# Layer 1's gathered rows in fp32 instead of three bf16 parts, in a two-layer graph network

## The chip, the cores and the metric

The kernel runs on one core of one Trainium2 chip. The metric is the device time of one execution, in microseconds (us), lower is better. Before the change it is 3567.8 us, the median of three runs (3565.1 to 3599.5). The core has a matrix engine (TensorE, PE in the profile, with its weight loads as PEld), a vector engine (VectorE, DVE), a scalar engine (ScalarE, ACT), GpSimd (POOL) and SyncE (SP), which issues transfers. Each works through its own list of instructions in order and waits for the others on semaphores.

## The reference, cut to what matters

There are 6250 nodes with 128 features each and 200,000 edges, sorted by their target node `dst`. The targets are drawn so that low node numbers have many edges.

```
h = relu(layernorm(x))
x = x + layer0(h, edges, edge_attr, edge_weight)     # a small network on each edge, summed by dst, + h
h = relu(layernorm(x))
agg = segment_sum(h[src], dst)                        # layer 1: the sum of the source rows of each node
x = x + relu(relu((h + agg) @ W1 + b1) @ W2 + b2)
```

The change lies in `agg` of layer 1 alone: a row of `h` is fetched for each edge and the rows of the edges that end at one node are added up.

## The kernel before

**Layout.** Edges go in blocks of 512 (4 tiles of 128), two blocks make a pair, four pairs a body (`RING = 4`). Node features lie as `nodes` and `xs`, 128 partitions by 49 tiles by 128 features (fp32); seven groups of seven tiles (`NG`, `GT`) are worked one after the other where whole arrays are passed over. `acc` holds the sums by node.

**Layer 0** takes the first 2575 us. In each pair GpSimd gathers 8 tiles of 128 rows from `table0` (fp32, 512 bytes a row) into the ring `big`; TensorE multiplies, VectorE adds, and the pair's messages are summed with a one-hot matrix `hot` in a product of fp32 operands (line 771: stationary 128x128 messages, 64 moving columns, the one-hot tile read as F32). Beside it counts of edges are made for dense windows (line 792).

**Between the layers** (lines 1239 to 1280 of VectorE, 655 to 675 of ScalarE, 836 to 855 of TensorE) the new `x` is formed, its layer norm made, and then, group by group:

- ScalarE writes the seven tiles of `nodes` (line 668, semaphore `normed1`), then copies the group to bf16 as the first part (line 675, `parts_first`); for the third group and later it waits until an earlier group's store has landed, as `parts` has two slots.
- VectorE subtracts that part (line 1268, `left_made`), GpSimd casts the remainder to bf16 as the second part (line 558), VectorE subtracts again and writes the third part in bf16 (line 1273, `parts_made`). The three parts add up to the fp32 value.
- TensorE transposes the group (line 850) and VectorE copies it to `acc` (line 1271, `acc1_made`).
- SyncE stores the parts as the group's rows of `table1`, 768 bytes a row (line 463).

GpSimd's gathers of layer 1 begin once all stores have landed (line 560) and `slot1_free` has its first four counts, which TensorE gives at line 855, after the last copy to `acc`.

**Layer 1's loop.** Nodes below 2880, with many edges each, are summed from the counts: `row_sums` (line 875) multiplies 49 tiles of `nodes` with counts, fp32, 49 products each time. The other edges, 16 bodies or 64 pairs, go by gathers. GpSimd gathers a pair (line 525, eight indirect transfers) when `slot1_free` says that TensorE is done with the pair four before (line 563). VectorE makes the pair's one-hot tiles (line 1061). TensorE's `sum_rows` (line 865) then multiplies each of the 8 gathered tiles with its one-hot tile: three bf16 products a tile, 24 a pair, each a weight load of 128x128 and 64 moving columns. VectorE adds the two sums to `acc` (line 1288), and makes the next pair's one-hot tiles only after that, as there is one set of them.

The order is written out by hand. A step of the loop over `k` (lines 897 to 907 and 1332 to 1342) has two bodies, so eight pairs, called slots t = 0 to 7. After its `sum_rows`, TensorE does in slots 0, 1 and 5 one `row_sums`; in slots 2 and 3 three windows of counts each, in slots 4, 6 and 7 two each (line 792, four bf16 products of 500 columns a window or more). Each window waits for one-hot tiles that VectorE makes in the same slot (lines 1133 and 1136), with room for half a window ahead of TensorE's. There are seven such steps, ahead of them one body with its own order (lines 890 to 896) and behind them one body of four pairs with nothing between the sums (lines 909 to 911). SyncE loads the indices of a later pair once a gather has landed (lines 466 to 472).

The last part multiplies with W1 and W2 and stores `out`.

Of the kernel before, what the change touches and what calls it, by code (L numbers as in the profile page):

```python
# [5 lines left out]
F32 = mybir.dt.float32  # L6
F32R = mybir.dt.float32r
BF16 = mybir.dt.bfloat16
F16 = mybir.dt.float16
I32 = mybir.dt.int32  # L10
ALU = mybir.AluOpType
ACT = mybir.ActivationFunctionType
AX = mybir.AxisListType

P = 128
D = 128
# [7 lines left out]
GT = 7  # L24
NG = NT // GT
N_PAD = NT * P
# [3 lines left out]
TB = 4  # L30
BLK = TB * P
RING = 4
NPAIR = -(-N_EDGES // (2 * BLK * RING)) * RING
NBODY = NPAIR // RING
NB = 2 * NPAIR
# [9 lines left out]
NBJ = NB // NBP  # L45
# [37 lines left out]

NP3 = 3


def gnn_program(nc, x, ea, ew, src, src_tiles, dst_tiles, dst_blocks, We1, be1, We2, be2, Wt, bt, Wn1, bn1, Wn2, bn2,
                W1, b1, W2, b2, out):
    ctx = ExitStack()
    with ctx:  # L90
        def sb(name, shape, dt=F32):
            return ctx.enter_context(nc.sbuf_tensor(name, shape, dt))

        def sem(name):
            return ctx.enter_context(nc.semaphore(name))

        def dram(name, shape, dt=F32):
            return nc.dram_tensor(name, shape, dt, kind="Internal").ap()


        table0 = dram("table0", (N_PAD, D))
        table1 = dram("table1", (N_PAD, NP3 * D), BF16)
        base_d = dram("base_d", (NB,), I32)
# [8 lines left out]
        nodes = sb("nodes", [P, NT, D])  # L112
# [49 lines left out]
        def one_hot_tiles(words, n):  # L162
# [34 lines left out]
        RROW = RING * 2 * TB * D  # L197
        big = sb("big", [P, RROW * NP3 // 2])
        assert RROW * NP3 // 2 == RROW + 2 * 2 * TB * D
        rows = big[:, 0:RROW].rearrange("p (u q t d) -> p u q t d", u=RING, q=2, t=TB)  # L200
        msg = big[:, RROW:RROW + 2 * 2 * TB * D].rearrange("p (m q t d) -> p m q t d", m=2, q=2, t=TB)
        rows1 = big[:, :].bitcast(BF16).rearrange("p (u q t i d) -> p u q t i d", u=RING, q=2, t=TB, i=NP3)

        parts = big[:, 0:2 * GT * D * NP3 // 2].bitcast(BF16).rearrange("p (s t i d) -> p s t i d", s=2, t=GT, i=NP3)
        left = big[:, GT * D * NP3:GT * D * NP3 + GT * D].rearrange("p (t d) -> p t d", t=GT)
        ef = sb("ef", [P, 2, BLK])
# [4 lines left out]
        half_at = RROW + 2 * TB * D - GT * D  # L211
        stages, stages2 = ([a[:, 0:GT * D].rearrange("p (t d) -> p t d", t=GT) for a in pair] for pair in (
            (big[:, RROW + 2 * TB * D:], big[:, half_at:]),
            (ef[:, :, :].rearrange("p q c -> p (q c)"), big[:, half_at - GT * D:])))
        assert NBJ * BLK + 2 * NB <= half_at - GT * D and GT * D * (NP3 + 1) <= RROW + 2 * TB * D

# [6 lines left out]
        hot = sb("hot", [P, 2, 2, TB, W], F32R)  # L223
        hot_sum = sb("hot_sum", [P, 2, 2, W], F32R)
        hot1 = hot[:, 0, 0, :, :].rearrange("p t w -> p (t w)").bitcast(BF16).rearrange("p (q t w) -> p q t w", q=2, t=TB)

# [7 lines left out]
        p_agg = ps[:, 7 * BANK:7 * BANK + 4 * W].rearrange("p (q s w) -> p q s w", q=2, s=2)  # L234
# [31 lines left out]
        table0_stored = sem("table0_stored")  # L266
        table1_stored = [sem(f"table1_stored{s}") for s in (0, 1)]

# [29 lines left out]
        normed1 = sem("normed1")  # L298
# [23 lines left out]
        rows_added = sem("rows_added")  # L322
        parts_first = sem("parts_first")
        left_made = sem("left_made")
        parts_second = sem("parts_second")
        parts_made = sem("parts_made")

# [39 lines left out]
        def _(sp):  # L367
# [35 lines left out]
            sweeps, start, total, bodies = load_params(sp)  # L403
# [57 lines left out]
            for g in range(NG):  # L461
                sp.wait_ge(parts_made, g + 1)
                sp.dma_start(t1[:, g * GT:(g + 1) * GT, :], parts[:, g % 2].rearrange("p t i d -> p t (i d)"))\
                  .then_inc(table1_stored[g % 2], 16)

# [33 lines left out]
        def _(pool):  # L499
# [30 lines left out]
            def gather_pair(table, to, u, landed):  # L530
                for q in (0, 1):
                    gather_block(table, to, u, q, landed)
# [3 lines left out]

            def to_rows1(u, q, t):
                return rows1[:, u, q, t].rearrange("p i d -> p (i d)")

            pool.wait_ge(table0_stored, 16 * NG)  # L540
# [14 lines left out]
            pool.tensor_copy(keys1, keys0).then_inc(keys_moved, 1)  # L555
            for g in range(NG):
                pool.wait_ge(left_made, g + 1)
                pool.tensor_copy(parts[:, g % 2, :, 1, :], left).then_inc(parts_second, 1)
            for s in (0, 1):
                pool.wait_ge(table1_stored[s], 16 * ((NG + 1 - s) // 2))  # L560
            with pool.Fori(0, total) as b:
                for u in range(RING):
                    pool.wait_ge(slot1_free, b * RING + u + 1)
                    pool.wait_ge(idx1_loaded[u], b * 16 + 16)
                    pool.sem_inc(pairs_begun, 1)
                    gather_pair(table1, to_rows1, u, gathered1)


        @block.scalar
        def _(act):  # L570
# [94 lines left out]
            for g in range(NG):  # L665
                for u in range(GT):
                    t = g * GT + u
                    i = act.activation(nodes[:, t, :],
                                       xs[:, t, :], ACT.Relu,
                                       bias=shift[:, t:t + 1], scale=rstd[:, t:t + 1])  # L670
                i.then_inc(normed1, 1)
                act.wait_ge(normed1, g + 1)
                if g >= 2:
                    act.wait_ge(table1_stored[g % 2], 16 * (g // 2))
                act.activation(parts[:, g % 2, :, 0, :], nodes[:, g * GT:(g + 1) * GT, :], ACT.Copy).then_inc(parts_first, 1)

# [35 lines left out]
        def _(pe):  # L712
# [144 lines left out]
            def sum_rows(b, u):  # L857

                n = b * (2 * RING) + 2 * u
                pe.wait_ge(hot1_made, n + 2)  # L860
                for q in (0, 1):
                    pe.wait_ge(gathered1[u][q], b * (16 * TB) + 16 * TB)
                    for t in range(TB):
                        for p in range(NP3):
                            i = pe.matmul(p_agg[:, q, 0, :], rows1[:, u, q, t, p, :], hot1[:, q, t, :],  # L865
                                          start=(t == 0 and p == 0), stop=(t == TB - 1 and p == NP3 - 1))
                i.then_inc(slot1_free, 1)
# [67 lines left out]
        def _(dve):  # L935
# [328 lines left out]
            for g in range(NG):  # L1264
                dve.wait_ge(parts_first, g + 1)
                if g:
                    dve.wait_ge(parts_made, g)
                dve.tensor_tensor(left, nodes[:, g * GT:(g + 1) * GT, :], parts[:, g % 2, :, 0, :], ALU.subtract)\
                   .then_inc(left_made, 1)
                dve.wait_ge(turned1, g + 1)  # L1270
                dve.tensor_copy(acc_group(g), p_turn[g % 2]).then_inc(acc1_made, 1)
                dve.wait_ge(parts_second, g + 1)
                dve.tensor_tensor(parts[:, g % 2, :, 2, :], left, parts[:, g % 2, :, 1, :], ALU.subtract)\
                   .then_inc(parts_made, 1)
            chain(dve.tensor_scalar(dense_edges, dst_t[:, :], float(C_NODES), -float(2 * N_PAD), ALU.is_lt, ALU.mult))
# [133 lines left out]
```

## Time and profile before

| | |
|---|---|
| median of three runs | 3567.8 us (3565.1 to 3599.5) |
| span of the profiled execution, first to last instruction | 3560.6 us |
| layer 0, to the last addition to `acc` | about 2575 us |
| layer 1's gathers, first to last | 2649.2 to 3501.8 us |
| TensorE busy | 2710.7 us, 76% |
| GpSimd busy | 2066.6 us, 58% |
| VectorE busy | 1969.1 us, 55% |
| mean granted TensorE clock | 0.80 of full speed |

The profile gives no whole time for the profiled execution beside its span; the median of the runs is 7.2 us above the span, and the fastest run 4.5 us. Busy shares are means over stages with different limits, so each stage is read by itself. One fp32 product of the program is two MATMUL and two LDWEIGHTS records in the trace (49 products of line 875 are 98 records), a bf16 product is one of each. A few records are missing. "Issue" in a wait means that the engine waited for nothing the profile shows.

### The profile page before, as it was taken

The numbers are of one execution on the slowest core, as the hardware profiler recorded it, in microseconds if no ns is written. First come the engines' busy times: TensorE is split into PE (matmuls) and PEld (weight loads), VectorE is DVE, ScalarE is ACT, GpSimd is POOL, SyncE is SP. The second block draws the span as 40 slices with busy tenths as digits, with TensorE's granted clock in tenths as the row PEclk, the third lists the DMA queues.
The fourth block names the chain that finished last, engine by engine and source line by source line (L and its number), as shares of the span: only waits on it lengthen the run. The fifth ranks groups of instructions, "written<-read, shape, count | busy, mean of one in ns | idle before, by whom it ended". The sixth has DMA issues, their size and how long they took to land. (4 is left out here: it accounts for less than half of the span.)

```text
span 3560.6 us, 56685 instructions
## 1 busy us (share of the span) xinstructions
PE 2710.7 (76%) x14584; PEld 1629.8 (46%) x14585; DVE 1969.1 (55%) x4112; ACT 1005.8 (28%) x1000; POOL 2066.6 (58%) x2104
## 2 busy tenths in 40 slices
PE   4677888788688888887888788887845767766777
PEld 2444444444344444444444444444432545544554
DVE  7655566565556666666666666676673333233333
ACT  3233333333333333333333333332241111111111
POOL 4666666656566666666666666655325556555552
PEclk8788888888888877888888888988765777777777
DMA  5444444444444444444444444434222434334332
GB/s 189 110 124 129 130 127 126 133 114 133 114 128 120 130 126 123 127 123 124 126 131 124 121 126 124 124 109 119 34 105 88 134 118 130 120 98 128 119 104 60
DMA packets 229238, 424.69 MB, mean 119 GB/s; under 512 B 82704, under 2 KB 141585, under 8 KB 229073
## 3 DMA queue, kind: packets, MB, share of 16 engines
q0 software_dynamic: 74752, 153.23, 18.4%
q1 hardware_dynamic: 103152, 177.42, 15.1%
q10 hardware_dynamic: 51266, 93.34, 7.5%
q8 instruction: 18, 0.29, 0.0%
q14 instruction: 50, 0.40, 0.0%
HBM read 364.35 MB, written 59.43 MB: 119 GB/s over the span
## 5 line engine op out<-in xcount | busy, mean ns | idle before, releaser
L525 POOL DMA_INDIRECT big<-table,idx x2080 | 2042.4, 982 | 1360.7 <-issue 670.2
L792 PE MATMUL ps<-nodes 128*128 128x500 bf16 x1280 | 467.5, 489 | 266.3 <-issue 170.5
L771 PE MATMUL ps<-hot,big 128*128 128x64 f32 x3136 | 419.0, 284 | 134.8 <-issue 111.1
L751 PE MATMUL ps<-arena,we 128*128 128x512 f32 x784 | 507.0, 778 | 14.2 <-issue 5.1
L604 ACT ACTIVATE big<-big 128x1024 f32<-128x1024 f32 x196 | 207.1, 1057 | 946.3 <-DVE big L1085 723.3
L771 PEld LDWEIGHTS ps<-hot,big 128*128 128x128 f32 x3136 | 402.4, 203 | 145.4 <-issue 143.0
L1136 DVE TENSOR_SCALAR nodes<-iota_k,win_off,nodes 128x500 bf16<-128x500 f16 x1280 | 454.7, 406 | 10.2 <-issue 10.1
L792 PEld LDWEIGHTS ps<-nodes 128*128 128x128 bf16 x1280 | 106.0, 109 | 520.1 <-issue 289.9
L1085 DVE TENSOR_TENSOR big<-ps,big 128x1024 f32<-128x1024 f32 x196 | 239.1, 1220 | 179.6 <-remote 121.3
L594 ACT ACTIVATE arena<-ps,cols 128x1024 f32<-128x1024 f32 x196 | 218.3, 1114 | 375.6 <-PE ps L743 160.4
L681 ACT ACTIVATE arena<-ps 128x490 f32<-128x490 f32 x96 | 100.0, 1041 | 754.6 <-PE ps L795 593.8
L1133 DVE TENSOR_TENSOR nodes<-iota_b,nodes 128x384 bf16<-128x384 f16 (+1 forms) x492 | 245.2, 498 | 112.6 <-remote 65.9
L627 ACT ACTIVATE arena<-ps 128x490 f32<-128x490 f32 x192 | 199.2, 1037 | 363.4 <-remote 345.4
L1105 DVE SCALAR_TENSOR_TENSOR arena<-ps,cols,arena 128x1024 f32<-128x1024 f32 x98 | 125.3, 1279 | 278.8 <-remote 262.8
L1078 DVE TENSOR_TENSOR acc<-ps,acc 128x128 f32 x392 | 113.7, 290 | 298.2 <-remote 237.9
L875 PE MATMUL ps<-acc,nodes 128*128 128x120 f32 x1568 | 221.5, 296 | 72.4 <-issue 65.2
L792 PE MATMUL ps<-arena 128*128 128x500 bf16 x384 | 171.9, 558 | 132.3 <-DVE arena L1136 92.7
L1133 DVE TENSOR_TENSOR arena<-iota_b,arena 128x256 bf16<-128x256 f16 x192 | 80.7, 421 | 317.1 <-PE ps L792 173.1
L743 PE MATMUL ps<-arena,we 64*128 64x512 f32 x784 | 233.5, 666 | 23.1 <-DMA win_row<-win_d 20.2
L875 PEld LDWEIGHTS ps<-acc,nodes 128*128 128x128 f32 x1568 | 207.4, 212 | 82.9 <-issue 82.6
L751 PEld LDWEIGHTS ps<-arena,we 128*128 128x128 f32 x784 | 171.3, 243 | 158.5 <-issue 153.7
L599 ACT ACTIVATE arena<-arena,cols 128x1024 f32<-128x1024 f32 x196 | 241.0, 1229 | 0.0
(139 smaller groups left out, 2577.0 us busy)
## 6 DMA issues: line engine op xcount, KB each, us to landing
arena<-in_ew SPq DMA_DIRECT2D x196, 512.0 KB
arena<-in_ea SPq DMA_DIRECT2D x196, 256.0 KB
counts_d<-arena ACTq DMA_DIRECT2D x192, 245.0 KB
acc<-counts_d ACTq DMA_DIRECT2D x15, 2940.0 KB
big<-table,idx POOLq DMA_INDIRECT x2080
table<-big SPq DMA_DIRECT2D x7, 672.0 KB, 3.0
idx<-in_src SPq DMA_DIRECT2D x260, 4.0 KB
xs<-in_x SPq DMA_DIRECT2D x7, 448.0 KB, 8.3
```

The source lines that it names most:

```text
L525: pool.indirect_dma_start(to(u, q, t), None, table, bass.IndirectOffsetOnAxis(ap=idx[:, u, at:at + 1], axis=0))\
L594: act.activation(hid[:, :, :].rearrange("p q c -> p (q c)"), p_hid2, ACT.Relu, bias=be1_c).then_inc(hid_made, 2)
L599: act.activation(v, v, ACT.Sigmoid, bias=bt_c, scale=wt_c).then_inc(tw_made, 2)
L604: act.activation(v, v, ACT.Relu).then_inc(msg_made, 2)
L743: pe.matmul(p_hid[q], we1[k, :], ea_s[k, u, :], start=True, stop=True).then_inc(hid_mm, 1)
L751: pe.matmul(p_ef[q], we2[:, :], hid[:, q, :], start=True, stop=True).then_inc(ef_mm, 1)
L771: pe.matmul(p_agg[:, q, 0, :], msg[:, m, q, t, :], hot_f[:, m, q, t, :], start=(t == 0), stop=(t == TB - 1))
L792: m = pe.matmul(to, hots[:, t, :], keys[:, t, :], start=False, stop=True, skip_group_check=True)
L875: m = pe.matmul(to, nodes[:, a, :], sums[:, :, a, :], start=(a == 0), stop=(a == NT - 1))
L1085: dve.tensor_tensor(msg[:, u % 2, :, :, :].rearrange("p q t d -> p (q t d)"), p_pre2, rows[:, u, :, :, :].rearrange("p q t d -> p (q t d)" ...
L1133: dve.tensor_tensor(hots[:, h * half:h * half + n, :], iota_v.to_broadcast([P, n, P]), half_src.to_broadcast([P, n, P]), ALU.is_equal)
L1136: m = dve.tensor_scalar(keys[:, h * half + t, :], iota_k[:, :], win_off[:, bass.ds(win, 1)], key[:, h * n + t:NTILE + VP][:, bass.ds(at, 1 ...
```

## The change

`table1` becomes fp32 with 512 bytes a row, and SyncE stores each group of `nodes` to it as soon as `normed1` says that it is written. ScalarE's copy to bf16, VectorE's two subtractions and GpSimd's cast are gone, with four semaphores, and the two store semaphores are one. GpSimd gathers fp32 rows into the same ring as layer 0. The one-hot tiles of layer 1 are fp32-sized (the tile `hot`, half of it), and `sum_rows` makes one fp32 product a tile, 8 a pair, with the same operands in form as line 771.

```diff
-        table1 = dram("table1", (N_PAD, NP3 * D), BF16)
+        table1 = dram("table1", (N_PAD, D))
...
-        hot1 = hot[:, 0, 0, :, :].rearrange("p t w -> p (t w)").bitcast(BF16).rearrange("p (q t w) -> p q t w", q=2, t=TB)
+        hot1 = hot[:, 0, :, :, :]
...
             for g in range(NG):
-                sp.wait_ge(parts_made, g + 1)
-                sp.dma_start(t1[:, g * GT:(g + 1) * GT, :], parts[:, g % 2].rearrange("p t i d -> p t (i d)"))\
-                  .then_inc(table1_stored[g % 2], 16)
+                sp.wait_ge(normed1, g + 1)
+                sp.dma_start(t1[:, g * GT:(g + 1) * GT, :], nodes[:, g * GT:(g + 1) * GT, :]).then_inc(table1_stored, 16)
...
-            for g in range(NG):
-                pool.wait_ge(left_made, g + 1)
-                pool.tensor_copy(parts[:, g % 2, :, 1, :], left).then_inc(parts_second, 1)
-            for s in (0, 1):
-                pool.wait_ge(table1_stored[s], 16 * ((NG + 1 - s) // 2))
+            pool.wait_ge(table1_stored, 16 * NG)
...
-                    gather_pair(table1, to_rows1, u, gathered1)
+                    gather_pair(table1, to_rows, u, gathered1)
...
-                act.wait_ge(normed1, g + 1)
-                if g >= 2:
-                    act.wait_ge(table1_stored[g % 2], 16 * (g // 2))
-                act.activation(parts[:, g % 2, :, 0, :], nodes[:, g * GT:(g + 1) * GT, :], ACT.Copy).then_inc(parts_first, 1)
...
-                        for p in range(NP3):
-                            i = pe.matmul(p_agg[:, q, 0, :], rows1[:, u, q, t, p, :], hot1[:, q, t, :],
-                                          start=(t == 0 and p == 0), stop=(t == TB - 1 and p == NP3 - 1))
+                        i = pe.matmul(p_agg[:, q, 0, :], rows[:, u, q, t, :], hot1[:, q, t, :].bitcast(F32),
+                                      start=(t == 0), stop=(t == TB - 1))
...
             for g in range(NG):
-                dve.wait_ge(parts_first, g + 1)
-                if g:
-                    dve.wait_ge(parts_made, g)
-                dve.tensor_tensor(left, nodes[:, g * GT:(g + 1) * GT, :], parts[:, g % 2, :, 0, :], ALU.subtract)\
-                   .then_inc(left_made, 1)
                 dve.wait_ge(turned1, g + 1)
                 dve.tensor_copy(acc_group(g), p_turn[g % 2]).then_inc(acc1_made, 1)
-                dve.wait_ge(parts_second, g + 1)
-                dve.tensor_tensor(parts[:, g % 2, :, 2, :], left, parts[:, g % 2, :, 1, :], ALU.subtract)\
-                   .then_inc(parts_made, 1)
```

## Rows read from the trace of the kernel before

**Rows 1.** Windows, three steps of layer 1's loop: us, PE, PEld, DVE, ACT, POOL, clock, DMA, GB/s.

```profile
2852.00:2955.00 103.00, 73.76 (x545) 51.06 (x546) 34.23 (x106) 12.04 (x12) 60.78 (x64) 0.73 0.38 114
2955.00:3060.00 105.00, 73.95 (x576) 52.51 (x573) 35.19 (x110) 12.95 (x13) 63.10 (x67) 0.73 0.41 126
```

**Rows 2.** Groups by line, layer 1's seven steps (2740 to 3496 us): busy, mean | idle before.

```profile
L525 POOL DMA_INDIRECT big<-table,idx x449 | 429.7, 957 | 327.3 <-issue 126.8 <-PE ps L865 119.8 <-remote 80.7
L865 PE MATMUL ps<-hot,big 128*128 128x64 bf16 x1344 | 75.0, 225 | 46.5 <-issue 26.2 <-DVE hot L1061 19.5
```

**Rows 3.** The chain of waits, 2968 to 3076 us, shares by line.

```profile
by line: PE ps L875 37.0%; issue 27.6%; PE ps L865 7.1%; PE ps L792 7.1%; DVE arena L1136 6.6%; DVEq L1116 4.2%; DVEq L1070 2.9%; DVEq L1133 2.5%; DVE arena L1133 1.5%; DVE hot L1061 1.3%; DVEq L1136 1.2%; DVE acc L1288 0.9%; DVEq L1140 0.6
```

**Rows 4.** Timeline of PE, one step: start, length, line, operands, count [idle before, releaser].

```profile
2969.19 1.46 PE L865 MATMUL ps<-hot,big 128*128 128x64 bf16 x24 [3.56 <-DVE hot L1061]
2970.46 12.56 PE L875 MATMUL ps<-arena,nodes 128*128 128x120 f32 x90
...
2986.45 0.86 PE L865 MATMUL ps<-hot,big 128*128 128x64 bf16 x24 [0.46 <-issue]
2987.14 11.18 PE L875 MATMUL ps<-acc,nodes 128*128 128x120 f32 x98
...
3008.59 1.46 PE L865 MATMUL ps<-hot,big 128*128 128x64 bf16 x24
...
3013.24 1.01 PE L792 MATMUL ps<-arena 128*128 128x500 bf16 x2 [3.08 <-issue]
...
3027.23 2.02 PE L792 MATMUL ps<-arena 128*128 128x500 bf16 x4 [4.20 <-DVE arena L1136]
...
3060.34 1.99 PE L792 MATMUL ps<-arena 128*128 128x500 bf16 x4 [1.53 <-issue]
```

**Rows 5.** Timeline of POOL in layer 1: gathers that follow a pair's last.

```profile
2988.12 0.94 POOL L525 DMA_INDIRECT big<-table,idx  x1 [3.40 <-PE ps L865]
...
2993.66 0.95 POOL L525 DMA_INDIRECT big<-table,idx  x1 [0.30 <-issue]
...
3014.31 1.05 POOL L525 DMA_INDIRECT big<-table,idx  x1 [2.38 <-remote]
```

**Rows 6.** Timeline of PE in layer 0, the fp32 product of line 771 and what follows it.

```profile
92.68 2.72 PE L771 MATMUL ps<-hot,big 128*128 128x64 f32 x16
95.20 0.25 PE L774 MATMUL ps<-hot_sum,ones 128*1 128x128 f32 x1
...
1501.00 1.90 PE L771 MATMUL ps<-hot,big 128*128 128x64 f32 x16
1502.71 0.25 PE L774 MATMUL ps<-hot_sum,ones 128*1 128x128 f32 x1
...
2571.77 3.02 PE L771 MATMUL ps<-hot,big 128*128 128x64 f32 x16 [1.56 <-DVE hot L1091]
2574.55 0.35 PE L774 MATMUL ps<-hot_sum,ones 128*1 128x128 f32 x1
```

**Rows 7.** Windows: granted clock (third from the end) around slots 0 and 1.

```profile
2963.00:2975.00 12.00, 7.92 (x50) 6.18 (x51) 3.01 (x11) 1.25 (x2) 7.40 (x8) 0.50 0.26 67
2975.00:2985.00 10.00, 8.63 (x76) 8.62 (x75) 0.94 (x3) 0.00 (x0) 7.56 (x8) 0.99 0.27 69
```

**Rows 8.** Timeline of all engines, from the first normalised group to the first gather.

```profile
2614.29 2.80 ACT L668 ACTIVATE nodes<-xs,shift,rstd 128x128 f32<-128x128 f32 x7 [0.78 <-DVE shift L976]
...
2640.18 1.76 PE L850 MATMUL ps<-ident,nodes 128*128 128x128 f32 x7 [2.02 <-ACT nodes L668]
...
2642.45 1.73 DVE L1271 COPY acc<-ps 128x896 f32<-128x896 f32 x1
2642.60 0.93 POOL L558 CAST big<-big 128x896 bf16<-128x896 f32 x1 [3.05 <-DVE big L1268]
2644.03 1.08 DVE L1273 TENSOR_TENSOR big<-big 128x896 bf16<-128x896 f32 x1
...
2649.18 0.97 POOL L525 DMA_INDIRECT big<-table,idx  x1 [5.65 <-issue]
```

**Rows 9.** Timeline of layer 1's last body: the first and the last pair's sums.

```profile
3510.76 0.87 PE L865 MATMUL ps<-hot,big 128*128 128x64 bf16 x24 [1.22 <-DVE hot L1061]
...
3518.81 1.46 PE L865 MATMUL ps<-hot,big 128*128 128x64 bf16 x24 [1.76 <-DVE hot L1061]
```

**Rows 10.** Groups by line: VectorE's one-hot tiles, layer 1's (256) and layer 0's (512).

```profile
L1061 DVE TENSOR_TENSOR hot<-ps,rel 128x256 bf16<-128x256 f32 x128 | 48.0, 416 | 22.4 <-issue 21.9 <-DVE ps L1278 0.3
L1091 DVE TENSOR_TENSOR hot<-ps,rel 128x512 fp32r<-128x512 f32 x6 | 4.1, 680 | 0.0
```

**Rows 11.** Timeline of POOL and PE in layer 0: a pair's first gather, and a slow stretch of TensorE.

```profile
1506.70 0.94 POOL L525 DMA_INDIRECT big<-table,idx  x1 [2.71 <-remote]
...
1562.59 1.34 PE L771 MATMUL ps<-hot,big 128*128 128x64 f32 x6 [0.50 <-issue]
```

More of the change, by code:

```diff
@@ L82 @@
 assert sum(SLOTS, ()) == tuple(range(CB))
-NP3 = 3
 def gnn_program(nc, x, ea, ew, src, src_tiles, dst_tiles, dst_blocks, We1, be1, We2, be2, Wt, bt, Wn1, bn1, Wn2, bn2,
@@ L197, in gnn_program @@
         RROW = RING * 2 * TB * D
-        big = sb("big", [P, RROW * NP3 // 2])
-        assert RROW * NP3 // 2 == RROW + 2 * 2 * TB * D
+        big = sb("big", [P, RROW + 2 * 2 * TB * D])
         rows = big[:, 0:RROW].rearrange("p (u q t d) -> p u q t d", u=RING, q=2, t=TB)
         msg = big[:, RROW:RROW + 2 * 2 * TB * D].rearrange("p (m q t d) -> p m q t d", m=2, q=2, t=TB)
-        rows1 = big[:, :].bitcast(BF16).rearrange("p (u q t i d) -> p u q t i d", u=RING, q=2, t=TB, i=NP3)
-        parts = big[:, 0:2 * GT * D * NP3 // 2].bitcast(BF16).rearrange("p (s t i d) -> p s t i d", s=2, t=GT, i=NP3)
-        left = big[:, GT * D * NP3:GT * D * NP3 + GT * D].rearrange("p (t d) -> p t d", t=GT)
         ef = sb("ef", [P, 2, BLK])
@@ L214, in gnn_program @@
             (ef[:, :, :].rearrange("p q c -> p (q c)"), big[:, half_at - GT * D:])))
-        assert NBJ * BLK + 2 * NB <= half_at - GT * D and GT * D * (NP3 + 1) <= RROW + 2 * TB * D
+        assert NBJ * BLK + 2 * NB <= half_at - GT * D
         dst_b = big[0:NBP, 0:NBJ * BLK].bitcast(I32).rearrange("p (j c) -> p j c", j=NBJ)
@@ L266, in gnn_program @@
         table0_stored = sem("table0_stored")
-        table1_stored = [sem(f"table1_stored{s}") for s in (0, 1)]
+        table1_stored = sem("table1_stored")
         ea_loaded = [sem(f"ea_loaded{u}") for u in range(RING)]
@@ L322, in gnn_program @@
         rows_added = sem("rows_added")
[L323 to L326, printed above, removed]
         hid2_mm = sem("hid2_mm")
@@ L535, in to_rows @@
                 return rows[:, u, q, t, :]
-            def to_rows1(u, q, t):
-                return rows1[:, u, q, t].rearrange("p i d -> p (i d)")
             pool.wait_ge(table0_stored, 16 * NG)
```

## The prediction, made before the result was known

> **What bounds the kernel now.** I read the share of busy time first and found no engine full, so the stage of the change has to be read by itself. The windows cut at layer 1's steps show about 105 us a step, with TensorE at 74, GpSimd at 61 to 63 and VectorE at 35 [rows 1]: again nobody is full, so the chain of waits and the timeline decide. GpSimd first, because the change touches its gathers. The grouped rows say that it waits 119.8 us for line 865, TensorE's sums of gathered rows [rows 2]; in the timeline it starts a pair's gathers 0.8 us after the sums that free the slot (sums from 2986.45 for 0.86 us, gather at 2988.12), and in the other pairs it is held back only by a gap of 2.4 us behind its own last gather [rows 4, 5]. It thus runs nearly a whole ring of four pairs ahead. Its floor is 8 gathers at 1.25 us (0.95 and a gap of 0.30) and 2.5 us between pairs, 12.5 us a pair or 100 us a step, 5 us under the present step. TensorE with VectorE sets the pace: on the chain of one step line 875 has 37.0%, "issue" 27.6%, line 865 and line 792 7.1% each [rows 3]. 7.1% of that window of 108 us is 7.7 us, and the sums are busy 75.0/7 = 10.7 us a step [rows 2], so about 70% of the sums' time is on the chain. That is the first sign of how much of a dearer sum will be felt.
>
> **Price of the fp32 sums.** Layer 0 has the very form that the change puts in: 128x128 fp32 stationary, 64 fp32 columns, the one-hot tile read as F32, 8 products or 16 records. I measure from its start to the start of what follows. At full clock (2.4 GHz) that is 1502.71 - 1501.00 = 1.71 us; at half (1.2 GHz) 2.52 (from 92.68) and 2.78 (from 2571.77), of which I take 2.6 [rows 6]. Three bf16 products a tile, 24 records, take 2987.14 - 2986.45 = 0.69 at full and 2970.46 - 2969.19 = 1.27 at half [rows 4]. So a pair gets dearer by **1.0 us at full and 1.3 at half clock** (ends: 1.0 and 1.5). Slot 0 lies in a stretch granted 0.50, and slot 1's follows one at 0.99 [rows 7].
> A rule of the Trainium skill speaks for a smaller price. The page "FP8 and Floating Point Precision", section "TensorE Precision Notes", says that a true fp32 product takes four passes through the array; against three bf16 products that would be 4/3 of the time. The row disagrees (1.71 against 0.69 is 2.5 times), so I hold to the row.
>
> **Where it is felt.** The order written out by hand decides it, slot by slot.
> - Slots 0, 1 and 5 have a row sum right behind, which waits for nothing (2970.46 and 2987.14 follow without a gap) [rows 4]: felt in full, 1.3, 1.0, 1.3.
> - Slots 2 and 6 have windows whose one-hot tiles VectorE has made during the row sum before: felt, 1.0 and 1.3. (That they are ready I read from the order, lines 1324 to 1326 against 898 to 907.)
> - In slots 3, 4 and 7 TensorE waits for VectorE behind the sums: 3.08, 4.20 and 1.53 us in this step [rows 4]. The smallest is over 1.3: felt at nothing. Without this cover it would cost 3 x 1.3 = 3.9 us a step.
> - In slot 0 the clock rises while TensorE works, and slot 1's row sum takes 11.18/98 = 114 ns a record, slot 0's, which begins at half clock, 12.56/90 = 140 [rows 4, 7]; a longer sum moves the row sum later, into the faster clock. I take 0.4 us off, ends 0 and 1.3.
> Sum: 1.3 + 1.0 + 1.0 + 1.3 + 1.3 - 0.4 = 5.5 us a step, **38.5 us** over seven. The last body has no cover: the first pair and the last run at 0.87 and 1.46 [rows 9], two pairs at each clock, 2 x 1.0 + 2 x 1.3 = 4.6. The first body I put at 1, between 0 (three of its sums are followed by waits for VectorE) and 5. Together **+44 us**.
>
> **The stage of the parts.** Now ScalarE's seven groups begin at 2614.29, the last third part is ready at 2644.03 + 1.08 = 2645.1 and the first gather starts at 2649.18, so a store takes 4.1 us to be seen [rows 8]. Afterwards ScalarE writes seven groups of 2.8 us without a stop and ends at 2633.9; plus 4.1 is 2638.0. The other condition of the gathers, TensorE's count of free slots, needs the last copy to `acc`: 2633.9, a transposition of 1.75 and the copy of 1.73, is 2637.4. What is late next is thus this copy, 0.6 us behind in line. Gain **11 us** at GpSimd. VectorE saves two subtractions of 1.08 a group and is 7.6 us earlier (2645.1 against 2637.5). The stored row sum that TensorE does first is stretched by the gathers beside it, so I take the 11, with 7.6 as the other end. Removed with it and off the chain: GpSimd's seven casts of 0.93, SyncE's stores shrink from 672 to 448 KB. SyncE now waits for `normed1` in place of `parts_made`; behind it stand only the next stores and later index loads, which need gathers to have landed. One store semaphore instead of two adds nothing.
>
> **Gathers and one-hot tiles.** A gather row shrinks from 768 to 512 bytes. GpSimd's time does not follow: 957 ns is its mean in layer 1 [rows 2], and layer 0 with 512-byte rows has 0.94 us and a gap of 2.71 between pairs [rows 11]. Nothing, as GpSimd is not the bound; if it became so, the same 12.5 us a pair. The one-hot tiles double in bytes, but VectorE writes 512 fp32 elements in 680 ns against 256 bf16 in 416 [rows 10], so the element costs 1.03 ns either way: nothing; the other end is 0.1 us a tile on the chain, 13 us over 128.
>
> **Slow stretches.** Beside gathers TensorE at times starts records some 0.7 us apart with no releaser ("issue"): 26.2 us in front of the sums in the seven steps [rows 2]. The sums' records fall by a third, 24 to 16; if each record costs its share, 9 us go. The lower end is nothing, and more is a rival below. I take **-9**.
>
> **The sum** is 44 - 11 - 9 = +24 us against the profiled span of 3560.6. The profile gives only this span, which lies 7.2 us under the runs' median; what lies around it does not change, so I add to the median: **3592 us**, +0.7%.
>
> **Rivals.**
> 1. *Every sum is felt* (ends slower). Place: slots 3, 4 and 7. If VectorE's windows do not start at their own time but as late after the sums as now, for example because both queues are slow at the same moment, the cover is none: 61 felt pairs at 1.35 are 82, and with a slow stretch that does not shrink, 82 - 11 = +71, **3639**. For it: the releaser of two of the three waits reads "issue" [rows 4], so their cause is not shown. Against: VectorE's windows do not wait for the sums in the code, and the chain has only 70% of line 865. It decides once more than 56 us of sums are felt, 47 if nothing else is saved. Chance 0.20.
> 2. *Sums at little price*, the rule of four passes as a mechanism here. 32 passes at the bf16 spacing would take 1.27 x 4/3 = 1.69 at half and 0.92 at full, +0.42 and +0.23: 1.7 a step, 12 in all, 1 for the last body, 13 - 11 - 9 = -7, **3561**. Against it stand all pairs of [rows 6]. Chance 0.12. (The page is the one named above.)
> 3. *Slow stretches follow the gathered bytes.* "Issue" is 27.6% of the chain [rows 3], 30 us a step. A third fewer bytes, a third fewer stalls: 10 a step, -70; 44 - 11 - 70 = -37, **3531**. Against: layer 0 gathers 512-byte rows, and there too a sum is torn apart by 0.50 us of "issue" and POOL has its 2.71 [rows 11]. It decides once 69 us of stalls go. Chance 0.13.
> That the product would not be fp32 at all is out: the operands are read as line 771's are, and that line shows two records a product.
> The forecast's own case: 0.55, from 3570 to 3612 (the ends of its terms).
>
> **Numbers.** What a measurement of this kernel can tell from no change is about 1%, 36 us: faster is under 3532, slower over 3603.5. Slower: rival 1 nearly whole and a third of my own case, 0.38. Faster: half of rival 3 and a little more, 0.08. The rest, 0.54, is within. The range for 8 in 10 leaves out the far half of rivals 1 and 3: **3548 to 3640**.
>
> **What would show it.** The sums at 1.9 us at full and about 2.8 at half clock in place of 0.86 and 1.46; the first gather 24 us behind ScalarE's first normalised group instead of 35; steps of 109 to 111 us; waits of TensorE for VectorE behind slots 3, 4 and 7 shrunk to between 0 and 3 us; GpSimd waiting longer for line 865. Wrong it would be with steps at 105 or under (rivals 2 and 3), with sums at 1.2 and 1.7 us (rival 2), or with those waits at their old length behind a longer sum (rival 1).

## The result and the profile after

The changed kernel takes **3641.8 us**, the median of four runs (3627.9 to 3654.5), beside 3566.5 for the kernel before (four runs). The ratio is 1.016, with a 95% interval of 1.011 to 1.022: slower, by 1.1 to 2.2%. The profiled execution has a span of 3652.7 us and is the slowest of the four, so a sum made from this trace overstates the median by some 13 us. The line numbers are 22 or 23 lower now: line 865 became 842, 875 became 852, 792 became 770.

I cut both traces at the same events. To ScalarE's first copy of `acc`, layer 0 takes 2581.7 us instead of 2575.8, which the change does not touch: +5.9. From there to the first gather 61.9 instead of 73.4: -11.5. From the first gather to the row sum that closes the first body 103.8 instead of 99.3: +4.5. From there to the start of the last row sum, which is seven steps, 832.4 instead of 747.6: **+84.8**, or 106.8 to 118.9 a step. The rest 72.9 instead of 64.6: +8.3. Together +92, the difference of the spans.

The groups of TensorE by line in the seven steps come first of the kernel before, where [rows 2] has the sums, then of the changed one (busy, mean of one | idle time before).

```profile
L875 PE MATMUL ps<-acc,nodes 128*128 128x120 f32 x1470 | 203.4, 294 | 44.2 <-issue 43.4
L792 PE MATMUL ps<-arena 128*128 128x500 bf16 x348 | 153.9, 552 | 116.0 <-DVE arena L1136 78.4 <-issue 37.3
L875 PE MATMUL ps<-arena,nodes 128*128 128x120 f32 x686 | 90.9, 295 | 6.6 <-issue 6.5
```

```profile
L852 PE MATMUL ps<-acc,nodes 128*128 128x120 f32 x1470 | 222.2, 315 | 55.3 <-issue 55.0
L842 PE MATMUL ps<-hot,big 128*128 128x64 f32 x896 | 161.3, 356 | 35.6 <-DVE hot L1038 29.1 <-issue 6.1
L770 PE MATMUL ps<-arena 128*128 128x500 bf16 x348 | 145.4, 528 | 84.4 <-DVE arena L1113 74.8 <-issue 9.1
L852 PE MATMUL ps<-arena,nodes 128*128 128x120 f32 x687 | 105.6, 318 | 18.8 <-issue 18.5
```

The sums went from 75.0 to 161.3 us busy, +86.3. The waits ahead of the windows gave 31.6 back and those ahead of the sums 10.9, and the windows themselves took 8.5 less. But the row sums, whose instructions nobody changed, took 33.5 us more of busy time and 23.3 more of waiting. That is the part no term of mine held.

One line of GpSimd and the chain of one step show who bounds the loop now. GpSimd waited 245.0 us for the sums instead of 119.8 [rows 2]: it has more slack, not less. In the chain the sums have 12.9% of 109 us, 14.1 us, instead of 7.7 [rows 3].

```profile
L514 POOL DMA_INDIRECT big<-table,idx x451 | 430.7, 955 | 410.4 <-PE ps L842 245.0 <-issue 129.6 <-remote 35.8
```

```profile
by line: PE ps L852 35.7%; issue 19.1%; PE ps L842 12.9%; DVE arena L1113 5.8%; PE ps L770 5.6%; DVEq L1047 3.8%; DVEq L1093 3.6%; DVE arena L1110 2.1%; DVE hot L1038 1.9%; DVEq L1113 1.7%; DVEq L1110 1.6%; DVE acc L1257 1.1%; DVEq L1102 1.
```

VectorE's one-hot tiles are not dearer in fp32, 416 ns each as in bf16 [rows 10]:

```profile
L1038 DVE TENSOR_TENSOR hot<-ps,rel 128x256 fp32r<-128x256 f32 x112 | 42.0, 416 | 21.6 <-issue 21.6
```

Then the sums themselves, in the timeline of TensorE after the change (start, length, ...). At full clock 16 records take 1.90 us, as I had read in layer 0 [rows 6]. At half clock they take 3.67, and 3.47 from their start to the start of what follows (3050.42 to 3053.89), where I had put 2.6.

```profile
3003.40 1.90 PE L842 MATMUL ps<-hot,big 128*128 128x64 f32 x16
3005.13 11.15 PE L852 MATMUL ps<-acc,nodes 128*128 128x120 f32 x98
...
3039.22 3.67 PE L842 MATMUL ps<-hot,big 128*128 128x64 f32 x16 [0.54 <-DVE hot L1038]
...
3045.80 1.99 PE L770 MATMUL ps<-arena 128*128 128x500 bf16 x4 [2.79 <-DVE arena L1113]
...
3050.42 3.67 PE L842 MATMUL ps<-hot,big 128*128 128x64 f32 x16
3053.89 10.44 PE L852 MATMUL ps<-acc,nodes 128*128 128x120 f32 x70
```

The rows from 3039 to 3046 show the cover at work: where TensorE waited 4.20 us for VectorE behind slot 4's bf16 sums [rows 4] it now waits 2.79 behind longer ones.

Last the start of the stage. The first gather comes 23.5 us behind the first normalised group (2643.65 - 2620.12) instead of 34.9 [rows 8]:

```profile
2620.12 18.96 ACT L650 ACTIVATE nodes<-xs,shift,rstd 128x128 f32<-128x128 f32 x49 [0.78 <-DVE shift L953]
...
2640.93 1.74 DVE L1243 COPY acc<-ps 128x896 f32<-128x896 f32 x1 [0.95 <-PE ps L828]
...
2643.65 2.50 POOL L514 DMA_INDIRECT big<-table,idx  x1 [55.73 <-PEq L833]
```

It was released by TensorE's count of free slots (line 833), which follows the last copy to `acc`, and not by the stores: this copy is indeed what is late next.

### The profile page after: what moved, and what is told of

The parts are those of the page before. It is cut to its first block, busy times and chain, and to the rows that moved or that the text cites. A ratio compares the mean times of both kernels' runs of the same rounds, so it can differ in the third digit from the quotient of the medians.

```text
span 3652.7 us, 55621 instructions
## 1 busy us (share of the span) xinstructions
PE 2817.5 (77%) x14072; PEld 1767.6 (48%) x14073; DVE 1959.1 (54%) x4098; ACT 997.7 (27%) x993; POOL 2056.8 (56%) x2097
## 4 chain that ended last, share of the span: by engine, by line
PE 36%; issue 19%; DVE 16%; DVEq 14%; another core or an unknown queue 13%; DMA 1%; ACT 1%; SPq 0%; ACTq 0%
PE ps L852 10%; PE ps L770 7%; PE ps L729 6%; DVE nodes L1113 5%; DVEq L1047 4%; PE ps L842 3%; PE ps L738 3%; PE ps L749 3%; DVEq L1093 3%; DVE hot L1068 2%; PE ps L721 2%; DVEq L1110 2%; DVEq L1113 2%; DVE arena L1113 2%
## 5 line engine op out<-in xcount | busy, mean ns | idle before, releaser
L770 PE MATMUL ps<-nodes 128*128 128x500 bf16 x1280 | 458.0, 480 | 271.3 <-issue 156.3
L729 PE MATMUL ps<-arena,we 128*128 128x512 f32 x784 | 496.3, 764 | 15.1 <-DVE arena L1082 5.6
L852 PE MATMUL ps<-acc,nodes 128*128 128x120 f32 x1568 | 239.4, 315 | 79.1 <-issue 74.1
L852 PEld LDWEIGHTS ps<-acc,nodes 128*128 128x128 f32 x1568 | 228.2, 231 | 87.5 <-issue 87.2
L738 PEld LDWEIGHTS ps<-wn1b,arena 128*128 128x128 f32 x1568 | 191.0, 197 | 115.0 <-issue 112.7
## 6 DMA issues: line engine op xcount, KB each, us to landing
counts_d<-arena ACTq DMA_DIRECT2D x192, 245.0 KB
```

The costliest lines, as they stand in the source:

```text
L729: pe.matmul(p_ef[q], we2[:, :], hid[:, q, :], start=True, stop=True).then_inc(ef_mm, 1)
L738: i = pe.matmul(p_pre[q][:, t * D:(t + 1) * D], efs[m][:, q, t * P:(t + 1) * P], wn1b[:, :], start=True, stop=True)
L770: m = pe.matmul(to, hots[:, t, :], keys[:, t, :], start=False, stop=True, skip_group_check=True)
L852: m = pe.matmul(to, nodes[:, a, :], sums[:, :, a, :], start=(a == 0), stop=(a == NT - 1))
```

## The experiments

All twelve kernels ran on three other chips, four on each, beside the kernel before on the same chip. There the kernel before takes 2899 to 2909 us and not 3567. GpSimd's eight gathers of a pair follow each other at 1.25 us with no gap of 2.4 us between pairs, and TensorE has next to no "issue" in front of its row sums (see the groups below). What makes the first chip's executions have these stretches was not found, and none of the twelve runs below was made on it. The prices of the product and of the cover could be measured all the same, on a loop without stalls.

**1 to 4: which part costs, and in which slots.** The first kernel undoes the product alone in the changed kernel:

```diff
-                        i = pe.matmul(p_agg[:, q, 0, :], rows[:, u, q, t, :], hot1[:, q, t, :].bitcast(F32),
-                                      start=(t == 0), stop=(t == TB - 1))
+                        for p in range(3):
+                            i = pe.matmul(p_agg[:, q, 0, :], hot1b[:, q, 0:2, :].rearrange("p t w -> p (t w)"), hot1b[:, q, t, :],
+                                          start=(t == 0 and p == 0), stop=(t == TB - 1 and p == 2))
```

> The changed kernel with three bf16 products a gathered tile again (24 a pair, 128x128 stationary, 64 columns); the stage of the parts stays away and the gathers stay at 512 bytes. Left out: the products read a one-hot tile as stationary operand in place of the gathered rows, so the sums of layer 1 are not the reference's. Theory A (all of the loss is the fp32 product): 3555 us, the old kernel less the 11 us of the stage that is gone. Theory B (the loss lies in the gathers, the one-hot tiles or the new start of the stage): stays over 3600.

Measured: 2896.8 us beside 2908.7, ratio 0.996 (0.994 to 0.997), **12 us faster** than the kernel before. The stage's gain is what I predicted, 11, and the smaller gathers leave no room for another effect. Theory B falls for the gathers and the stage. The fp32 one-hot tiles go with the fp32 product in every kernel here, so these runs do not part the two; the 416 ns above do.

The second does the product alone in the kernel before:

```diff
-                        for p in range(NP3):
-                            i = pe.matmul(p_agg[:, q, 0, :], rows1[:, u, q, t, p, :], hot1[:, q, t, :],
-                                          start=(t == 0 and p == 0), stop=(t == TB - 1 and p == NP3 - 1))
+                        i = pe.matmul(p_agg[:, q, 0, :], rows_f[:, u, q, t, 0:D], hot1[:, q, t, :].bitcast(F32),
+                                      start=(t == 0), stop=(t == TB - 1))
```

> The old kernel with its stage of parts and 768-byte rows, and one fp32 product a tile (it reads the first 512 bytes of a row of parts as fp32, so the sums are not the reference's). Theory A: 3567 + 86 (the whole measured loss of 75 and the 11 that the missing stage gave) = 3653 us. Theory B: near 3567.

Measured: 2989.0 us, ratio 1.026 (1.023 to 1.029), **+80 us**. Theory A stands: 768-byte rows and the parts stage are there and the loss is too. With the 12 us of the stage off, the two kernels give +68.

The third and fourth choose the product by slot (`if fp32` around the two forms, and the one-hot tiles to match). The diff is the third's; the fourth has `(0, 1, 2, 5, 6), True`, where `True` puts the fp32 product in the first and last body too:

```diff
+FP32_SLOTS, OUTER = (3, 4, 7), False
...
-                    sum_rows(k * 2 + (t // RING - 1), t % RING)
+                    sum_rows(k * 2 + (t // RING - 1), t % RING, t in FP32_SLOTS)
```

> As the kernel with bf16 products again, but the fp32 product in slots 3, 4 and 7 of the step alone (seven steps), where TensorE waited for VectorE behind the sums. Cover theory: an fp32 sum at half clock is 2.2 us dearer than the bf16 one, the waits were 3.1, 4.2 and 1.5 us, so 0.7 us a step is felt: 5 us over the kernel with bf16 products. Rival, every sum is felt: 3 x 2.2 x 7 = 46 us over it.

> The other part: fp32 products in slots 0, 1, 2, 5, 6 and in the first and last body, bf16 in slots 3, 4 and 7. Cover theory: nearly the whole loss, 75 to 80 us over the kernel with bf16 products. Rival, every sum is felt alike: 7 x (2 x 2.2 + 3 x 1.0) + 11 = 63 or less, about 40 under the changed kernel.

Measured: 2901.5 us for slots 3, 4, 7, which is 4.7 over the kernel with bf16 products everywhere, where the cover theory said 5 and its rival 46. And 2957.6 us for the others, 60.8 over it (57 by the ratios), less than the 75 to 80 of the cover theory and near the 63 of its rival. The two add up to 65 us. The cover theory thus holds for the third kernel and misses the fourth; the table below shows what it lacked.

**5 to 8: the changed kernel on such a chip, and two ways on.**

> The changed kernel itself, on the chip of these runs. On a chip where GpSimd needs 10 us a pair and the old kernel 2909 us, the parts measured so far add up: 57 (slots 0, 1, 2, 5, 6 and the outer bodies) + 5 (slots 3, 4, 7) - 13 (no stage of parts) = +49 us or 1.7%. If the slots' parts do not add (a wait moved from one slot to the next), it is 20 us or more off that.

Measured: 2969.5 us beside 2899.3, ratio 1.025 (1.023 to 1.027): **+70 us** and not 49. The slots' parts do not add; over the kernel with bf16 products it is some 83, by the medians 82, and the two parts gave 65. The next table says where. It holds the mean time from one slot's sums to the next slot's, over the seven steps, worked out from the timelines of TensorE:

```
slot                          0      1      2      3      4      5      6      7    step
first chip, before        15.04  17.51   8.50  12.47  10.24  19.41   6.98  16.82  107.0
first chip, after         20.61  17.59   8.74  13.86  10.35  25.32   6.27  16.39  119.1
bf16 products             13.49  11.81   7.61  10.77   7.72  13.50   5.38  12.91   83.2
fp32 in slots 3, 4, 7     13.37  11.75   7.62  11.29   8.31  13.06   5.34  12.99   83.7
fp32 in the others        15.74  12.73   8.48  10.72   7.72  15.87   6.28  13.06   90.6
changed kernel            16.11  12.73   8.47  11.34   8.35  16.90   6.27  13.11   93.3
```

In the last four rows each slot can be read by itself. Slots 1, 2 and 6 grow by 0.9, the price at full clock. Slots 3 and 4 grow by 0.6 and slot 7 by 0.2 where their sums grow by 2.2, 2.2 and 1.0: the cover holds most of it in every kernel. The traces show it directly: TensorE's waits inside these three slots are 2.20, 1.77 and 2.67 us in the mean with bf16 products and 0.67, 0.49 and 1.70 in the changed kernel. Slots 0 and 5 grow by 2.6 and 3.4. Slot 5 is where the parts do not add: -0.4 with fp32 in slots 3, 4 and 7, +2.4 with fp32 in slot 5 itself, +3.4 with both.

So the price of slots 3, 4 and 7 depends on what the others run. With bf16 in the others, fp32 in these three makes a step 0.5 us longer (83.2 to 83.7). With fp32 in the others it makes it 2.7 us longer (90.6 to 93.3), 19 us over the seven steps, and 1.4 of the 2.7 appear in slots 5 and 0.

The timelines of slot 5 show where. First the kernel with bf16 products, then the one with fp32 products in the others, slot 5 among them, then the changed one. The row sum of 98 records behind the sums takes 12.40, 12.29 and 13.60.

```profile
2396.63 1.46 PE L844 MATMUL ps<-hot 128*128 128x64 bf16 x24
2397.91 12.40 PE L854 MATMUL ps<-acc,nodes 128*128 128x120 f32 x98
2410.14 0.86 PE L844 MATMUL ps<-hot 128*128 128x64 bf16 x24
```

```profile
2408.00 3.68 PE L845 MATMUL ps<-hot,big 128*128 128x64 f32 x16
2411.47 12.29 PE L859 MATMUL ps<-acc,nodes 128*128 128x120 f32 x98
2423.60 1.90 PE L845 MATMUL ps<-hot,big 128*128 128x64 f32 x16
```

```profile
2401.25 3.67 PE L842 MATMUL ps<-hot,big 128*128 128x64 f32 x16
2404.72 13.60 PE L852 MATMUL ps<-acc,nodes 128*128 128x120 f32 x98
2418.16 1.90 PE L842 MATMUL ps<-hot,big 128*128 128x64 f32 x16
```

And the windows over the same three stretches, from the sums to the end of the row sum (granted clock third from the end): 0.87, 0.81 and 0.74 on average.

```profile
2397.00:2410.00 13.00, 13.00 (x118) 13.00 (x116) 3.16 (x10) 0.68 (x1) 9.81 (x11) 0.87 0.21 51
```

```profile
2408.00:2423.00 15.00, 15.00 (x109) 15.00 (x110) 3.16 (x10) 1.04 (x1) 11.34 (x13) 0.81 0.19 48
```

```profile
2401.00:2418.00 17.00, 16.97 (x115) 16.85 (x115) 3.35 (x11) 1.04 (x1) 12.37 (x13) 0.74 0.18 53
```

The clock is at half first and at full after that, so these shares tell when it rises: 3.8, 5.8 and 8.6 us after the start of slot 5's sums. The second kernel does what I had assumed with my 0.4 us off: its sums are 2.2 us longer, the clock rises 2.0 later, and in five of its seven steps the row sum is a little shorter than with bf16 sums (12.3 against 12.4 to 12.6); in the other two it took 12.7 and 13.8, so this is no fixed amount. In the changed kernel the sums of slot 5 are no longer than that, and yet the rise comes 2.8 us later still. What differs is slots 3, 4 and 7 before it. That their longer sums and shorter waits move the rise is thus shown; which of them does it, and why, was not tried.

The filler kernels put products whose results nobody reads where TensorE waits:

```diff
+            def fill(n):
+                for i in range(n):
+                    pe.matmul(ps[:, 4 * BANK:4 * BANK + CK], iota_b[:, :], iota_k[:, :], start=True, stop=True)
...
+                    if t in (3, 4, 7):
+                        fill(3)
                     for i in SLOTS[t]:
                         count_late(k, i)
+                    if t == 7:
+                        fill(7)
```

> The changed kernel with filler products (128x128 by 500 columns, 16 bit, result never read) where TensorE waited for VectorE: 3 behind the sums of slots 3, 4 and 7, and 7 ahead of slot 0. Theory (the sums of slots 0, 3, 4, 5, 7 cost 3.7 us and not 1.9 because the granted clock is half there): the clock stays up, those sums take 1.9, and it is 30 to 60 us faster than the changed kernel. Rival (the clock does not follow, or the fillers themselves are in the way): the fillers add up to 7 x 16 x 0.42 = 47 us less what the waits hide, 0 to 30 us slower.

> The same fillers in the old kernel. Its step is near GpSimd's floor on a chip with 10 us a pair: nothing, within 10 us. On a chip with 12.5 us a pair TensorE sets the pace and the sums cost only 1.27 against 0.69: 10 to 25 us faster if the clock follows.

Measured: 2962.4 us, ratio 1.022 (1.019 to 1.024), 7 us under the changed kernel. The two intervals overlap, but on this chip each run of the one (2954.8 to 2966.0) lies under each of the other (2968.6 to 2971.9). Neither the 30 to 60 us of the theory nor the rival's range holds it. The fillers gave 2884.1 us in the kernel before, ratio 0.995 (0.993 to 0.997), **15 us faster**, where I had expected nothing on such a chip. The clock follows in some places only. The sums of slots 4 and 5 stay at 3.67 in the mean, slot 0's go from 3.42 to 2.86. In a step where the clock has risen by then, slot 0's sums take 1.99, as here, where seven fillers at line 852 run in the wait:

```profile
2523.74 2.95 PE L852 MATMUL ps<-iota_k,iota_b 128*128 128x500 f16 x7
2527.01 1.99 PE L842 MATMUL ps<-hot,big 128*128 128x64 f32 x16 [0.32 <-DVE hot L1046]
2528.84 1.33 PE L856 MATMUL ps<-arena,nodes 128*128 128x120 f32 x10
```

In the mean slots 0 and 5 gain 1.0 and 1.1 us and slots 3 and 4, where the fillers run longer than the wait, lose 0.8 and 1.3 in the changed kernel. That a sum costs 1.90 us where the granted clock is 1.00 and 3.67 where it is 0.50 is shown by every kernel; that the half clock can be bought off with fillers at this price is not.

The next kernel splits each row into two bf16 parts instead of three. It leaves out the third part (and with it GpSimd's cast) and holds about 16 of the value's bits:

```diff
-NP3 = 3
+NP3 = 2
...
-                dve.tensor_tensor(left, nodes[:, g * GT:(g + 1) * GT, :], parts[:, g % 2, :, 0, :], ALU.subtract)\
-                   .then_inc(left_made, 1)
+                dve.tensor_tensor(parts[:, g % 2, :, 1, :], nodes[:, g * GT:(g + 1) * GT, :], parts[:, g % 2, :, 0, :], ALU.subtract)\
+                   .then_inc(parts_made, 1)
```

> The old kernel with two bf16 parts instead of three: 512-byte rows, 16 bf16 products a pair, no GpSimd cast and one subtraction less a group. It holds 16 bits of the value, not 24. Where TensorE sets the pace: sums a third shorter, 7 x 5 x 0.35 = 12 us, and the stage 6 to 8 us shorter: 20 us under the old kernel. Where GpSimd sets the pace: the stage alone, 8 us.

Measured: 2882.1 us, ratio 0.994 (0.992 to 0.997), **17 us faster** than the kernel before: it beats both. That is nearer the 20 I gave for a chip where TensorE sets the pace than the 8 for one where GpSimd does.

**9 to 12: does GpSimd's floor hide anything?** A step of the kernel with bf16 products is 83 us, near the 80 that GpSimd needs for eight pairs at 10 us. Perhaps its floor, and not the wait for VectorE, had made slots 3, 4 and 7 so cheap, and the parts did not add for that reason. These kernels gather half of the tiles, so the floor is 40:

```diff
-                    gather_block(table, to, u, q, landed)
+                    gather_block(table, to, u, q, landed, TB // 2)
...
-                    pe.wait_ge(gathered1[u][q], b * (16 * TB) + 16 * TB)
+                    pe.wait_ge(gathered1[u][q], b * (8 * TB) + 8 * TB)
```

> The changed kernel with bf16 products, and layer 1 gathers only 4 of the 8 tiles of a pair, so GpSimd's floor (8 x 1.25 = 10 us a pair, 80 a step) is halved. Left out: half of layer 1's rows, and the products read the one-hot tile. Floor theory: the bf16 kernel stood at 81.7 us a step because GpSimd's 80 us held it, so it gets 2 us a step or more faster, 15 to 40 us in all under the old kernel less 13. Rival, TensorE and VectorE held it as well: within 5 us of the kernel with bf16 products and all gathers.

> The changed kernel with 4 of 8 gathers a pair in layer 1 (half of the rows left out). Floor theory: TensorE sets its pace anyway (92 us a step over the floor of 80), so it stays within 10 us of the changed kernel, and its distance to the bf16 kernel with half gathers is the full busy time of the fp32 sums, 80 to 90 us. Rival: the distance stays at 70 to 75.

> fp32 products in slots 3, 4 and 7 alone, with 4 of 8 gathers a pair. If GpSimd's floor hid these sums when they were tried with all gathers (5 us felt where the difference of the other two kernels leaves 28), 20 to 35 us over the bf16 kernel with half gathers. If the waits for VectorE hid them, 5 again.

Measured beside 2906.4: 2885.9 us with bf16 products (ratio 0.994, 0.992 to 0.996), 2972.4 with fp32 ones (1.022, 1.020 to 1.024), 2889.5 with fp32 in slots 3, 4 and 7 (0.994, 0.992 to 0.996). The bf16 kernel gains 0.2% by the ratios, 5 us, over its form with all gathers, which is within the intervals (by the medians less the kernel before on each chip it is 9); its step is 83.0 instead of 83.2. So the floor theory falls, by its own numbers for the first and the third: slots 3, 4 and 7 cost 3.7 us with the floor out of the way. Only the distance of the fp32 kernel to the bf16 one, 86.6 us, lies in the 80 to 90 that it gave, and that hardly differs from the 83 with all gathers. The waits for VectorE are the cover, as in the code. Nor is the floor the reason why the parts do not add: with half the gathers slots 5 and 0 of the changed kernel are as long as before (16.95 and 16.22 us).

> Two bf16 parts with the filler products. Both changes alone gave 0.5 to 0.6% on the old kernel. Where GpSimd's floor is near they do not add in full: 20 to 28 us under the old kernel, 0.7 to 1.0%.

Measured: 2888.4 us, ratio 0.994 (0.992 to 0.996), 18 us under the kernel before. That is the gain of two parts alone, under the 20 to 28 expected: the fillers add nothing clear to it. None of these faster forms was run on the first chip.

## Why the prediction came out as it did

The forecast was +24 us, within 1%, with slower at 0.38; it became +75 in the medians (+58 by the ratio). The median of 3641.8 lies 1.8 us over the range's upper end of 3640; by the ratio the time is 3626, inside it and outside my own case, which ended at 3612. What bounds the loop, the cover and the stage of parts were as forecast. The price of a sum at half clock was too small, and the growth of the row sums had no term. The first rival stood at 3639, but its mechanism did not bring the time there.

- **Who bounds.** Right. TensorE with VectorE sets the pace, GpSimd waits for the sums still more afterwards, and halving its gathers changes next to nothing.
- **Price of the fp32 sums.** Right at full clock (1.7 us, +1.0), wrong at half: 3.47 and not 2.6, so +2.2 a pair and not +1.3. The two rows I read it from [rows 6] were not at half clock from end to end; the windows over them give a mean granted clock of 0.70 and 0.68. Layer 0 also has a sum that was, with a window at 0.50: it takes 330.63 - 327.22 = 3.41.

```profile
92.00:96.00 4.00, 4.00 (x24) 3.72 (x23) 3.90 (x4) 0.27 (x1) 3.21 (x3) 0.70 0.14 34
2571.00:2575.00 4.00, 3.13 (x17) 2.87 (x17) 1.70 (x3) 0.00 (x0) 0.00 (x0) 0.68 0.01 4
```

```profile
327.22 3.65 PE L771 MATMUL ps<-hot,big 128*128 128x64 f32 x16 [3.96 <-DVE hot L1091]
330.63 0.35 PE L774 MATMUL ps<-hot_sum,ones 128*1 128x128 f32 x1
```

```profile
327.00:331.00 4.00, 3.78 (x18) 3.59 (x18) 3.90 (x8) 2.88 (x3) 2.83 (x3) 0.50 0.68 172
```

  Twice the full-clock 1.71 is 3.4 too. Slot 6 I had put at half clock; its fp32 sums ran at full in every trace (1.90). With 2.2, 2.2 and 1.0 slots 0, 5 and 6 of my sum give 5.4 and not 3.9 a step, 10.5 us over seven steps.
- **Where it is felt.** Right for each slot's own time: slots 1 and 2 in full, 3, 4 and 7 at 0.6, 0.6 and 0.2, even with the larger price. But a forecast slot by slot has no place for what slots 3, 4 and 7 do to slots 5 and 0, which makes their price 19 us in the changed kernel and not the 4 to 5 they cost alone. On the first chip slots 1, 2 and 6 came out at +0.1, +0.2 and -0.7, since their bf16 sums had been stretched by stalls (2.5, 1.24 and 2.32 us in the mean) and the fp32 ones (2.18, 2.04, 1.90) less or not at all.
- **The clock behind slot 0.** My 0.4 us off holds behind slot 5 where slots 3, 4 and 7 stay bf16. In the changed kernel the row sums of slots 0 and 5 become longer instead, by 0.6 and 1.2 us in the mean on the chips without stalls.
- **Slow stretches: -9.** This step failed. "Issue" in front of the sums did fall, by 20 us (26.2 to 6.1), and in front of the windows by 28 (37.3 to 9.1). But in front of the row sums it rose by 23.6, most of it inside those of slots 0 and 5 (+11 and +9), where nothing covers it. Both slots grew by 5.6 and 5.9 us a step on the first chip against 2.6 and 3.4 elsewhere. A row sum of slot 5 shows such a stretch; it ends soon after the pair's last gather has been issued at 3303.14:

```profile
3292.41 7.27 PE L852 MATMUL ps<-acc,nodes 128*128 128x120 f32 x38
3301.41 0.26 PE L852 MATMUL ps<-acc,nodes 128*128 128x120 f32 x1 [1.73 <-issue]
3302.85 0.26 PE L852 MATMUL ps<-acc,nodes 128*128 128x120 f32 x1 [1.17 <-issue]
3303.56 0.36 PE L852 MATMUL ps<-acc,nodes 128*128 128x120 f32 x1 [0.45 <-issue]
3305.64 0.36 PE L852 MATMUL ps<-acc,nodes 128*128 128x120 f32 x1 [1.72 <-issue]
3306.36 8.96 PE L852 MATMUL ps<-acc,nodes 128*128 128x120 f32 x56 [0.36 <-issue]
```

  The windows over it show what the waits alone do not: in the stretch TensorE is busy 2.54 of 6 us at a granted clock of 1.00, and behind it the clock is back at 0.50, so that the 56 records at the end take 160 ns each and not 114.

```profile
3298.00:3304.00 6.00, 2.54 (x17) 1.92 (x15) 1.59 (x4) 0.00 (x0) 4.64 (x5) 1.00 0.20 55
3305.00:3311.00 6.00, 5.00 (x23) 4.87 (x23) 0.00 (x0) 0.00 (x0) 0.00 (x0) 0.50 0.02 2
```

  Inside the row sums of slot 0 the clock falls a second time in 4 of 7 steps (none before), inside those of slot 5 in 6 of 7 (3 before). Together these row sums are at half clock for 131 us instead of 45 and last 277 instead of 224, which is 53 of the 84.8 us. On a chip without stalls the clock falls a second time in none of them, with bf16 products or fp32. That the stretches lie under the row sums because the longer sums shifted these against the gathers is my reading and was not tried: no run of mine beside the first two met such stretches. Their cause stays open.
- **The stage of the parts: -11.** Right, 11.5 in the trace and 12 in the kernel that changes only this.
- **Outer bodies: +5.6.** Too small: +4.5 and +8.3. In the last body one pair of the four ran at full clock and three at half, where I had two and two, at the larger price. In the first body there is also an "issue" wait of 7.99 us in front of a window, which is not the price of a sum.

Of the rivals, the first (no cover in slots 3, 4, 7) is refuted by two experiments, though its sum of 3639 is close to what was measured. The second, sums at little price, is refuted by every sum in the trace: 1.90 and 3.67 us, where 4/3 of the bf16 sums' 0.86 and 1.46 would be 1.15 and 1.95. The third needed 69 us of stalls to go with a third of the bytes. The changed kernel still has 88.7 us of TensorE's "issue" in the four groups shown, where the kernel before had 113.4 with [rows 2]; 24.7 went, and more of what is left lies where it is felt.

## What to carry to other kernels

Before a price is taken from a row at "half clock", read the granted clock over just that row: a burst that straddles a change of clock looks like a mild price and hides the real one. And place a dearer operation slot by slot: three of eight slots here took 1.0 to 2.2 us more work at 0.2 to 0.6 us of their own time, while the ones ahead of an uncovered fp32 row sum cost more than their own growth. Then look again at the whole step, since a covered sum is not free when it moves a later rise of the clock: these three cost 0.5 us a step alone and 2.7 beside the others. At these shapes (128x128 stationary, 64 moving columns) splitting fp32 rows into three bf16 parts pays, since a pair's 24 bf16 products took 1.27 us at half clock against 3.47 for its eight fp32 ones; two parts pay a little more where their precision suffices.

## What the runs showed of the hardware that I had not expected

- The same kernel takes 3567 us on one chip and 2899 to 2909 us on three others. It was not profiled on the others, but the traces of all twelve kernels there lack the "issue" stretches and GpSimd's 2.4 us between pairs. Most of the difference lies in layer 0: ScalarE's first copy of `acc` comes at 2581.7 us in the changed kernel on the first chip and at 2116.0 on another. Four groups by line of the changed kernel's steps on such a chip, to be held against those above:

```profile
L852 PE MATMUL ps<-acc,nodes 128*128 128x120 f32 x1470 | 185.7, 291 | 4.8 <-DVEq L1274 4.8
L842 PE MATMUL ps<-hot,big 128*128 128x64 f32 x880 | 152.5, 346 | 36.0 <-DVE hot L1038 27.0 <-DMA big<-table,idx 8.1
L770 PE MATMUL ps<-arena 128*128 128x500 bf16 x344 | 146.0, 542 | 38.6 <-DVE arena L1113 37.7
L852 PE MATMUL ps<-arena,nodes 128*128 128x120 f32 x686 | 91.4, 301 | 0.0
```

- How late the clock rises behind the same sum of 16 fp32 records at half clock (3.67 us of busy TensorE) depends on what ran before that sum. With bf16 sums and longer waits in slots 3, 4 and 7 it rose 5.8 us after the sum's start in five of seven steps, and 98 fp32 records behind it took 12.3 us. With fp32 sums there it rose 8.5 to 8.7 us after it, and they took 13.6.
- On the first chip TensorE's clock fell back to half inside a row sum of 98 records in 10 of 14 row sums of slots 0 and 5, in the shown one behind a stretch in which single records started about 0.7 to 2 us apart.
- Seven fillers of 500 columns in the wait ahead of slot 0's sums brought these to their full-clock length in part of the steps only (2.86 us in the mean instead of 3.42).
